# Layer 0 of a two-layer gated cross-attention kernel: scores and maxima in two row tiles of 64 partitions

## The reference

```python
# layer 0, cross attention (b = 16 batches, 56 queries, 1500 keys, 16 heads of 8)
q = split_heads(query @ Wq.T + bq)          # query = layernorm(x)
k = split_heads(key @ Wk.T + bk)            # key = value = ctx_1024
v = split_heads(value @ Wv.T + bv)
scores = jnp.einsum('bhqd,bhkd->bhqk', q, k) / np.sqrt(HEAD_DIM)
weights = jax.nn.softmax(scores, axis=-1)
out = jnp.einsum('bhqk,bhkd->bhqd', weights, v)
# layer 1 is the same but for
scores = jnp.where(m == 0, jnp.float32(-1000000000.0), scores)
# around them
x = x + jnp.tanh(g_xattn[l]) * xattn_l(_layernorm(x), ctx_1024, ctx_1024, ...)
x = x + jnp.tanh(g_ffn[l]) * ffn_l(_layernorm(x), ...)    # 8 experts, top 2
```

## Time and profile before

| | us |
|---|---|
| three runs | 1040.19, 1042.14, 1044.49 (median 1042.14) |
| the profiled execution | 1040.89 |
| its span | 1039.0 |
| PE busy in it | 926.1 (89%) |
| DVE busy | 720.9 (69%) |
| ACT busy | 586.6 (56%) |
| POOL busy | 525.0 (51%) |

### The profile page before, as it was taken

The page is one execution under the profiler, slowest core; times in us unless marked ns, Lnnn a source line. Parts: engine busy times, 40 slices in busy tenths (PEclk is TensorE's granted clock), DMA queues, the critical chain, the costliest instruction groups (busy, mean ns, idle before and its releaser), DMA issues.

```text
span 1039.0 us, 32346 instructions
## 1 busy us (share of the span) xinstructions
PE 926.1 (89%) x13088; PEld 679.7 (65%) x13088; DVE 720.9 (69%) x1531; ACT 586.6 (56%) x1060; POOL 525.0 (51%) x667
## 2 busy tenths in 40 slices
PE   2587899999999999999999999999999999999974
PEld 0154577777877777777777777666666666666753
DVE  2476676785767767586785877877787878787722
ACT  1044557556565555656557565665757675757560
POOL 5352445543546334453546665666657666662202
PEclk9998999999999999999999999999999999999995
DMA  8745653333323333233465656767676667665200
GB/s 180 134 89 136 145 132 67 80 75 69 76 43 85 70 82 71 43 76 69 99 133 93 138 114 130 160 129 154 125 155 120 144 127 148 132 138 100 49 2 18
DMA packets 95216, 107.26 MB, mean 103 GB/s; under 512 B 22394, under 2 KB 86972, under 8 KB 95068
## 3 DMA queue, kind: packets, MB, share of 16 engines
q1 hardware_dynamic: 95068, 105.19, 49.1%
HBM read 35.89 MB, written 0.46 MB: 35 GB/s over the span
## 4 chain that ended last, share of the span: by engine, by line
PE 66%; DVE 16%; ACT 9%; issue 5%; SPq 2%; DMA 1%; POOL 0%; POOLq 0%; ACTq 0%; DVEq 0%
PE pO L993 13%; PE pMX L1010 12%; PE pST L972 12%; PE pKV L1122 6%; PE pFY L1082 6%; PE pKV L1115 5%; PE pFH L1148 5%; DVE mx L925 4%; DVE mx L920 4%; ACT P L678 3%; DVE rden L839 3%; PE pFY L1047 2%; ACT HR L715 1%; PE pFY L1086 1%; ACT V L696 1%
## 5 line engine op out<-in xcount | busy, mean ns | idle before, releaser
L678 ACT ACTIVATE P<-pST 125x448 f32<-125x448 f32 x768 | 396.3, 542 | 347.8 <-PE pST L972 342.6
L925 DVE TENSOR_REDUCE mx<-pMX 112x1 f32<-112x500 f32 x384 | 258.5, 673 | 174.4 <-PE pMX L1010 173.9
L1010 PE MATMUL pMX<-kop,qmax 104*112 104x500 f16 x768 | 292.9, 392 | 42.4 <-DMA qmax<-qlo 17.3
L972 PE MATMUL pST<-qexp,kop 106*128 106x112 f16 (+1 forms) x3072 | 280.2, 215 | 19.9 <-ACT P L678 9.3
L972 PEld LDWEIGHTS pST<-qexp,kop 106*128 106x128 f16 (+1 forms) x3072 | 210.1, 102 | 126.9 <-issue 42.5
L920 DVE TENSOR_REDUCE mx<-pMX 112x1 f32<-112x500 f32 x384 | 255.8, 666 | 42.1 <-PE pMX L1010 41.0
L993 PE MATMUL pO<-P,V 125*17 125x112 f32 x6144 | 186.0, 262 | 0.0
L993 PEld LDWEIGHTS pO<-P,V 125*17 125x17 f32 x6144 | 136.8, 98 | 46.0 <-issue 36.3
L1010 PEld LDWEIGHTS pMX<-kop,qmax 104*112 104x112 f16 x768 | 99.2, 132 | 91.3 <-issue 21.7
L563 POOL CAST khi<-kfull 128x500 f16<-128x500 f32 x96 | 57.7, 601 | 193.2 <-ACT kfull L691 193.0
L565 POOL TENSOR_TENSOR klo<-kfull,khi 128x500 f16<-128x500 f32 x96 | 109.0, 1135 | 7.8
(11 more groups left out here) (144 smaller groups left out, 1131.3 us busy)
## 6 DMA issues: line engine op xcount, KB each, us to landing
C<-in_ctxT SPq DMA_DIRECT2D x32, 750.0 KB, 6.2
kop<-khi SPq DMA_DIRECT2D x192, 125.0 KB
kop<-maskop SPq DMA_DIRECT2D x48, 437.5 KB
kop<-klo SPq DMA_DIRECT2D x96, 125.0 KB
qexp<-qmax SPq DMA_DIRECT2D x32, 182.0 KB
maskin<-in_mask SPq DMA_DIRECT2D x8, 656.2 KB, 6.8
kop<-maskop SPq DMA_DIRECT2D x2, 1312.5 KB
qmax<-qhi SPq DMA_DIRECT2D x128, 7.0 KB
```

What stands on the lines that cost most here:

```text
L678: nc.scalar.activation(P[0:KP, slot, h * 4 * T:(h + 1) * 4 * T], pST[0:KP, h, 0:4 * T], ACT.Exp, scale=EXP_SCALE).then_inc(exp_done, 1)
L925: nc.vector.tensor_reduce(mx[:, s % 2, m // PAIRS, m % PAIRS:m % PAIRS + 1], pMX[0:T, 1, 0:CW], AX.X, ALU.max).then_inc(max_done, 1)
L972: mm = nc.tensor.matmul(pST[0:cols, h, i * T:(i + 1) * T], kop[0:ROWS, b, p, tile * KP:tile * KP + cols], qexp[0:ROWS, b, p, :, :].rearran ...
L1010: nc.tensor.matmul(pMX[0:T, m % 2, 0:CW], qmax[0:SHIFT0, st.s % 2, p, :, :].rearrange("r j q -> r (j q)"), kop[0:SHIFT0, st.s % 2, p, c * ...
```

## The change

In layer 0 the mask rows are left out. A pair then needs 48 rows for the maxima and 50 for the scores, which fits into 64 partitions: pairs 0 to 3 lie on partitions 0 to 49 and pairs 4 to 7 on partitions 64 to 113 of the same columns. The weights of layer 0 are permuted so that the projections put out the keys and queries in that order. Both maxima of a tile step are issued together, one in each row half, and the eight scores of a tile step follow them, alternating between the halves. Since both banks are filled at once, the scores of a tile step wait for both exponentials of the one before. SP copies each half with a DMA of its own. Layer 1 keeps its layout and its order. The mask rows of layer 1 come with its own copies; its shift rows and query mask rows are written as batches 16 and 17 are prepared.

```diff
+SHIFT0_L0 = 3 * PR
+ROWS_L0 = SHIFT0_L0 + 2
+HALF = 64
+HP = PAIRS // 2
...
+def pair_at(n, m):
+
+    c, i = divmod(m, PAIRS)
+    return (c, HP * (i % 2) + i // 2) if layer_of(n) == 0 else (c, i)
...
             for b in range(2):
-                sp.dma_start(kop[MASK0:SHIFT0, b, :, :],
-                             maskop[0:S, :].unsqueeze(1).broadcast_to([S, PAIRS, S2])).then_inc(init_dma, 16)
-                for i in range(2):
-                    sp.dma_start(kop[SHIFT0 + i:SHIFT0 + i + 1, b, :, :],
-                                 shift_rows[:, i:i + 1, :].broadcast_to([1, PAIRS, S2])).then_inc(init_dma, 16)
-                sp.dma_start(qmax[MASK0:SHIFT0, b, :, :, :],
-                             pick[:, :, :].rearrange("s (p j) q -> s p j q", j=2)).then_inc(init_dma, 16)
+                for h in range(2):
+                    row = HALF * h + SHIFT0_L0
+                    sp.dma_start(kop[row:row + 2, b, 0:HP, :].rearrange("r p (i n) -> r (p i) n", n=SHW),
+                                 shift_rows[:, :].unsqueeze(1).broadcast_to([2, HP * S2 // SHW, SHW])
+                                 ).then_inc(init_dma, 16)
...
                 for row, part in ((0, khi), (PR, klo), (2 * PR, khi)):
-                    sp.dma_start(kop[row:row + PR, dst, :, cols], part[:, cols]).then_inc(kop_in[c], 16)
+                    if n < B:
+                        for h in range(2):
+                            at = HALF * h + row
+                            sp.dma_start(kop[at:at + PR, dst, 0:HP, cols], part[HALF * h:HALF * (h + 1), cols]
+                                         ).then_inc(kop_in[c], 16)
...
                         for j in range(2):
+                            if s + 1 < B:
+                                for h in range(2):
+                                    at, of = HALF * h + row + HD * j, HALF * h + HALF // 2 * j
+                                    sp.dma_start(qmax[at:at + HD, (s + 1) % 2, 0:HP, j, :],
+                                                 part[of:of + HALF // 2, half:half + S]).then_inc(qmax_in, 16)
...
+            def score_rows(st, kt):
+
+                back, tile = tile_at(kt, E_LAG)
+                n = st.s - back
+                if not is_batch(n) or layer_of(n) == 1:
+                    return
+                b, keys = score_operands(n, tile)
+                if n > 0 or tile > 0:
+                    pe.wait_ge(exp_done, 2 * (KT * n + tile))
+                for i in range(HP):
+                    for h in range(2):
+                        rows = slice(HALF * h, HALF * h + ROWS_L0)
+                        mm = nc.tensor.matmul(pST[0:keys.stop - keys.start, h, i * T:(i + 1) * T],
+                                              kop[rows, b, i, keys],
+                                              qexp[rows, b, i, :, :].rearrange("r j q -> r (j q)"),
+                                              start=True, stop=True)
+                        if i == HP - 1:
+                            mm.then_inc(st_ready, 1)
...
+                if layer_of(n) == 0:
+                    h, i = divmod(p, HP)
+                    rows, slot = slice(HALF * h, HALF * h + SHIFT0_L0), i
+                else:
+                    rows, slot = slice(0, SHIFT0), p
+                nc.tensor.matmul(pMX[0:T, m % 2, 0:CW], qmax[rows, b, slot, :, :].rearrange("r j q -> r (j q)"),
+                                 kop[rows, b, slot, c * CW:(c + 1) * CW], start=True, stop=True).then_inc(mx_ready, 1)
...
+                    if together:
+                        max_scores(st, m0)
+                        max_scores(st, m0 + 1)
+                    if not experts:
+                        score_rows(st, kt)
+                    if apart_ and not late:
+                        max_scores(st, m0)
                     weigh(st, kt)
-                    experts = [u[1] for u in fy_uses(s) if u[0] == kt and early(u[1])]
                     if experts:
                         small("y0")
-                        if has_m(s):
-                            max_scores(st, MAXES_PER_KT * kt + 1)
+                        if apart_:
+                            max_scores(st, m0 + 1)
                         small("y1")
+                        score_rows(st, kt)
                     score_half(st, kt, 0)
```

223 lines of the change are left out of this document (137 added, 86 removed).

## The result

The changed kernel takes 1095.9 us (median of four runs, 1094.8 to 1099.7), the kernel before 1043.3 beside it: 1.051 times as long, 95% interval 1.047 to 1.054. The forecast was 1064, with a range of 1047 to 1080. The sign held; 22 us were forecast, and it is 53, so the time lies above the range and above the 1092 of the 8-in-10 range too.

The account below looks back on a forecast made before the run. PE's list was taken as the bound. 1039.0 us of span plus 15 (six pairs of steps at 2.5), 1 and 7.5 for SP gave 1062.5; on the scale of the runs about 1065, stated as 1064, range 1047 to 1080.

Parts of the forecast that it names:

- 8-in-10 range: Whole kernel: 1028 to 1092 us, the forecast's range with the far ends left out.
- Overlap: PE, layer 0: row halves fully side by side, a pair of maxima in 0.22 us, eight scores in 0.20.
- Changes of shape: PE, at a new tile shape: 0.09 to 0.11 us a change, plus 0.05 us for the first weight load.
- the rival: Layer 0's tiles don't overlap: 3.7 us a step more, 1108 us; no or half overlap or clock, above 1080: 0.18.
- Waits added, 7.5 us: PE, two steps of layer 0: scores behind copies 4.5 us, maxima behind reductions 1.5, short tile steps 1.5.
- saved work, 5.0: PE, two steps of layer 0: 5.0 us less work from paired maxima and scores, changes of shape counted in.
- SP and the start: SP's doubled issues: first maxima 4 us earlier, at 33, but step 4 7 to 8 us late; +7.5 us taken, 0 to +13.
- Step 16: Steps 1 to 3, 16 and 17 have part of the steady steps' loss, together 1 us.
- The granted clock: Rival: clock falls in layer 0 as PE idles more, tens of us; not expected; with no or half overlap 0.18.

Follow-up runs that it names:

- run 1: Kernel before with its own layout and copies, but layer 0 in the changed order (both maxima together, then eight scores behind one wait): 1081.6 us, ratio 1.033.
- run 13: Changed kernel with the late weights issued in the middle of the next step, behind the shifts, instead of at a step's end: 1085.1 us, ratio 1.034.
- run 6: Changed kernel with each pair of layer 0's maxima computed twice in a row: 1102.7 us, ratio 1.055.
- run 12: Changed kernel with each row half's products contracting over all 64 rows, the unused query rows being zeros: 1085.5 us, ratio 1.036.
- run 5: Kernel before's order and copies (four small ones more at the start), layer 0's products over 48 and 50 rows in one row half: 1110.8 us, ratio 1.062.
- run 3: Changed kernel with both of ACT's exponentials in layer 0 ahead of the copy of the projection: 1067.1 us, ratio 1.023.
- run 17: Kernel before with late weights moved behind the shifts and products on constant data keeping PE busy in early steps: 1039.6 us, ratio 0.995.
- run 4: Changed kernel without the second row half's copies of keys and queries from batch 2 on: 1088.9 us, ratio 1.040.
- run 2: Changed layout and copies, but layer 0 in the order and with the separate waits of the kernel before: 1117.4 us, ratio 1.070.

## Why the prediction was half right

The direction and the steady steps at the full clock came as reckoned. The size did not: times above 1080 had a chance of 0.18, for tiles that don't overlap or for the clock, and it was the clock.

- **Overlap** (likeliest: full): right. 0.25 us for two maxima, 0.21 for eight scores (0.22 and 0.20 taken). The Trainium skill (TensorE: Matmul & The Clock Gate, Measured speedup vs the span model) adds about 4 ns for each further tile; the scores agree with their 0.21 against 0.20 us, the maxima cost ten times that, 0.04 us.
- **Changes of shape** (0.09 + 0.05 us): right. 4.5 and 5.2 us in two steps in the runs without overlap (4.6 in the rival). The Trainium skill (TensorEngine Tiling (Array Packing), Key Properties) says that a change of the tiling mode drains the engine. The trace agrees: behind the eight scores at 455.51 us the first projection starts 0.30 us later, where maxima of the same tile size start 0.21 later (465.22 to 465.43).
- **Waits added, 7.5 us, and saved work, 5.0**: their difference was right, 2.2 us in two steps at 1.00 for 2.5, but by luck. The order alone costs 4.75 us (run 1) and the packing takes 2.6 off it, so by these both terms were some 2.5 us too large. PE's waits in steps 5 to 15 grew by 23.7 us, 4.3 in two steps, and without the waits behind copies two steps are 2.5 us shorter, not 4.5.
- **The first rival's sum**: its 3.7 us a step is less than its own parts, 2.3 for changes of shape and half of 7.5 for waits, which make 6.0. No run has both without overlap; apart they cost 4.5 and 4.75 us in two steps, 4.6 a step together.
- **SP and the start**: the step was right and too small. First maxima came at 30.32 us (33 forecast), issues cost 0.62 us, and the shifts came late behind the late weights. Step 4 started 11.6 us late, not 7.5, inside the 0 to 13 allowed, and lost 6.4 us more itself, where 1.3 were forecast. The doubled issues by themselves are worth 7 to 8 us, the order of the late weights 11, with step 4's loss in both.
- **Step 16**: missed. I gave steps 1 to 3, 16 and 17 together 1 us; step 16 alone takes 3.7 us more at 1.00, 3.0 of which go when ACT's exponentials come first.
- **The granted clock**: this is the step that failed. I wrote that it "is 1.00 in steps 7 and 8, and waits of 0.9 us between products are too short for me to expect it" to fall, and left it to the upper tail. At 1.00 steps 5 to 15 would take 6 x 31.51 + 5 x 34.12 = 359.7 us; they took 372.5: 12.8 us. Step 17 adds 2.5 (32.87 at 0.90, 30.34 before). That is 15 of the 31 us by which the span exceeds its forecast of 1062.5. Step 16 is another 3.7 and the end of the program 5.0 (0.75 against 0.82), which I can't lay to the change. Steps 0 to 4 are 9 us worse than forecast; there waits for SP and the low clock come together. (All of these make 33 us; 1.7 by which steps 5 to 15 at 1.00 came in under their forecast and the 1 us given for steps 1 to 3, 16 and 17 go off.) Run 13 shows that part of both goes with the place of the late weights, and I can't part them further.

What the runs showed in its place: the change lowered the clock in two ways. It took work from PE and left waits (run 6 gives work back, and in steps 5 to 15 the time at the lower level falls from 31 to 3 us), and it filled less of the array per product (run 12 fills the halves, with the same steps otherwise, and it falls to 10 us; run 5 points the same way, but changes more than rows). That waits alone do it is refuted by run 1. I did not try which of the two counts more, whether the changes of shape have a part of their own, nor why single executions of one kernel differ in where their slow stretches lie; with the end's 82 or 87 us, which runs with the same layer 1 show alike (82.3 in run 3, 87.3 in run 13, and 87.3 in run 17, whose layer 0 is that of before), such placing is worth 5 us and is no effect of layer 0's layout that I could show.

## What to carry to other kernels

Work taken from the matrix engine that leaves its waits in place can lower its clock; reckon the steady step at both levels, and read the granted clock of every stretch before taking 1.00 for given. If side-by-side tiles leave rows unused, fill them with zeros and time it; here it gave 10 us, and some 3, within the noise, once the waits were repaired. When two banks are filled at once, look at what the engine that empties them does in between: moving one copy behind the second exponential was worth 29 us in all, and at the full clock 2.5 us in two steps, as much as the packing itself (2.6).

## What the hardware showed that was not expected

- In these traces PE is at its lower level up to the first clock entry, and the rows say 1.00 there because they count missing entries as 1.00. In run 5 the first entry is at 89.1 us, in the kernel before at 54.2, in the one after at 52.5, in run 4 at 89.4. Value projections of run 5 around it:

```profile
88.74 0.31 PE L1128 MATMUL pKV<-Wlo,Chi 128*125 128x128 f16 x1
88.84 0.31 PE L1128 MATMUL pKV<-Whi,Clo 128*125 128x128 f16 x1
...
89.06 0.23 PE L1128 MATMUL pKV<-Wlo,Chi 128*125 128x128 f16 x1
89.12 0.22 PE L1128 MATMUL pKV<-Whi,Clo 128*125 128x128 f16 x1
```

  Products of 128 columns start 0.10 to 0.11 us apart and then 0.06, as the 0.058 of the earlier trace rows: half speed, 1.2 GHz, up to the entry, and 2.4 GHz from there. Run 4 has the same at 78 to 90 us under a row that says 1.00:

```profile
78.00:90.00 12.00, 10.41 (x128) 7.35 (x118) 3.28 (x7) 4.38 (x9) 4.50 (x6) 1.00 0.07 21
```

  The distance of like products is the surer sign, and the 1.00 of step 1 in runs 2 and 5 must be read so.
- Zeros in unused rows, no more columns and no more products, took 10 us off (run 12, 1085.5 for 1095.9).
- Moving late weights within SP's list, two issues of 3.13 us together ahead of step 4's shifts, changed PE's clock in step 4 from 0.83 to 1.00 (run 13).
